# Edge ids broadcast to all partitions by DMA, and a softplus that ends in one instruction, in a graph network kernel

## What is computed

```
h = relu(layernorm(x))
f = (softplus(edge_attr @ W1 + b1) - log 2) @ W2 + b2      # per edge
x = x + segment_sum(h[dst] * f, src)                       # layer 0
h = relu(layernorm(x))
for k in (1, 2):                                           # layer 1, two convolutions
    agg[n, r] = mean of h[src] over the edges with dst = n and type = r
    h = sum over r of agg[:, r] @ Wrel[r] + h @ root + bias    # a relu after the first
x = x + h
```

## Time and profile before

| | us |
|---|---|
| median of 3 runs | 7747.99 (7746.06 to 7757.31) |
| the profiled execution | 7740.94 |
| its span, first to last instruction | 7739.2 |
| busy in the span: PE / PE weight loads | 4879.2 / 3639.4 |
| busy in the span: DVE / ACT / POOL | 3524.5 / 3186.8 / 5938.5 |

### The profile page before, as it was taken

How to read it: one execution, slowest core, us unless ns; L and a number is a source line. 1 busy time by engine, 2 the same in 40 slices (tenths; PEclk the granted TensorE clock), 3 DMA queues, 4 the chain that set the end, 5 groups by cost and what they waited for, 6 DMA issues and landing times. The chain is left out here.

```text
span 7739.2 us, 134678 instructions
## 1 busy us (share of the span) xinstructions
PE 4879.2 (63%) x27214; PEld 3639.4 (47%) x27214; DVE 3524.5 (46%) x10829; ACT 3186.8 (41%) x8459; POOL 5938.5 (77%) x5311
## 2 busy tenths in 40 slices
PE   1877777777777777686666666666644444444444
PEld 1656655665555556544444444444433333333333
DVE  6555555555555555486555555555521111111111
ACT  5555555555555555474333333333322222222222
POOL 4888888888888888846777777777767777777777
PEclk9988888888888888896666666666655555555555
DMA  8555555555555555584222222222222222222222
GB/s 262 86 84 84 84 84 84 84 83 84 84 84 84 84 84 84 70 304 134 70 80 80 78 79 80 77 80 80 77 61 56 56 56 56 56 56 56 56 56 54
DMA packets 587140, 663.53 MB, mean 86 GB/s; under 512 B 109683, under 2 KB 448091, under 8 KB 586755
## 3 DMA queue, kind: packets, MB, share of 16 engines
q0 software_dynamic: 352384, 340.33, 27.3%
q1 hardware_dynamic: 228934, 314.99, 12.9%
q10 hardware_dynamic: 5746, 7.42, 0.4%
HBM read 406.44 MB, written 255.87 MB: 86 GB/s over the span
## 5 line engine op out<-in xcount | busy, mean ns | idle before, releaser
L1321 POOL DMA_INDIRECT got<-table_dram,cidx x3328 | 3150.6, 947 | 1056.0 <-issue 1003.3
L980 POOL DMA_INDIRECT acc_dram<-total,idx x1664 | 2600.2, 1563 | 563.9 <-issue 361.1
L1369 PE MATMUL bank<-got,share 128*128 128x128 f32 x6656 | 1604.4, 417 | 1529.0 <-DMA got<-table_dram,cidx 1493.1
L1369 PEld LDWEIGHTS bank<-got,share 128*128 128x128 f32 x6656 | 1379.0, 307 | 1808.5 <-issue 1702.2
L1423 ACT ACTIVATE share<-cto_node,etcol 128x128 f32<-128x128 bf16 x3328 | 1082.5, 396 | 2756.3 <-PE bank L1369 1863.3
L240 DVE SCALAR_TENSOR_TENSOR xs<-bank,mask_hi,xs 128x128 f32 x416 | 146.0, 351 | 1681.6 <-PE bank L1369 1681.6
L946 DVE TENSOR_TENSOR msg<-bank,factor 128x512 f32<-128x512 f32 x416 | 287.8, 692 | 1219.1 <-issue 889.7
L871 ACT ACTIVATE total<-bank 128x258 f32<-128x258 f32 x832 | 275.5, 384 | 1200.4 <-DMA acc_dram<-total,idx 1200.4
L814 PEld LDWEIGHTS bank<-w,soft 128*128 128x128 f32 x3328 | 569.0, 242 | 33.1
L805 PE MATMUL bank<-msg,same 128*128 128x129 f32 x3328 | 583.9, 328 | 0.7 <-issue 0.7
L797 PE MATMUL bank<-rows,coef 2*128 2x512 bf16 x416 | 170.7, 410 | 653.1 <-DVE same L953 652.7
(11 more groups left out here) (178 smaller groups left out, 7667.1 us busy)
## 6 DMA issues: line engine op xcount, KB each, us to landing
edges<-in_edge_attr SPq DMA_DIRECT2D x415, 256.0 KB
got<-table_dram,cidx POOLq DMA_INDIRECT x3328
table_dram<-made SPq DMA_DIRECT2D x98, 512.0 KB, 3.7
table_dram<-umade SPq DMA_DIRECT2D x98, 512.0 KB, 2.9
win<-split_dram SPq DMA_DIRECT2D x416, 96.0 KB
acc_dram<-total,idx POOLq DMA_INDIRECT x1664, 3.3
acc_dram<-zeros SPq DMA_DIRECT2D x132, 192.0 KB, 2.8
sums<-acc_dram SPq DMA_DIRECT2D x196, 64.0 KB, 3.2
```

The lines of the kernel that those rows point to most:

```text
L980: pool.indirect_dma_start(g.acc_dram[j][:, :], bass.IndirectOffsetOnAxis(ap=idx[k][:, j:j + 1], axis=0), total[k][:, j, 0:F], None, comput ...
L1321: pool.indirect_dma_start(got[k][:, j, :], None, g.table_dram[which][:, :], bass.IndirectOffsetOnAxis(ap=idx[k][:, j:j + 1], axis=0)).then ...
L1369: ins = nc.tensor.matmul(window[k], share[k][:, j, :], got[ka][:, j, :], start=j == 0, stop=j == TG - 1)
```

## The change

The id row reaches all partitions by DMAs that read the same row of DRAM 128 times. In the filter layer the source ids come as int32 from the input itself (`src_row`), and the low parts of the target ids come as bf16 from `rows_dram` (`low`). `to_edge` compares the low part with `want`, the low part of the node number of the partition; within a window of 128 nodes the low parts are distinct. The last group, which the input does not fill, takes its source ids from `last_dram`, which `prepare` writes. The source parts aren't made or stored any more. In the softplus, max(z + b1, 0) = max(z, -b1) + b1: one DVE instruction computes max(z, -b1) + log1p from PSUM, and the missing b1 is added to `neglog`, so that it comes back through the second bias. `bank_z` alternates between two PSUM banks, since the bank is read until that last instruction. The first convolution takes its ids in the same way. For inputs in which a group doesn't fit its window, the matmul for the target stays.

```diff
 # prepare
-            def store_rows(k):
+            def store_rows():
+            sp.wait_ge(s_ids[1], 16 * PIECES)
+            sp.dma_start(g.last_dram.rearrange("(a e) -> a e", a=1), ids[1][QP - 1:QP, EQ - GE:EQ]).then_inc(s_last, 16)
...
             scales(0)
+            dve.wait_ge(s_weights, 16 * 12)
+            v.tensor_scalar(neglog[:, :], neglog[:, :], g.b1c[:, 0:1], None, ALU.add).then_inc(s_neglog, 1)
+            chain(v.tensor_scalar(g.neg_b1[:, :], g.b1c[:, :], -1.0, None, ALU.mult))
...
-            id_parts(1)
             to_floats(1)
...
             chain(v.tensor_copy(g.ctl[:, :], fits[:, :]))
+            chain(v.tensor_scalar(off_f[:, :], g.neg_nid[:, :], -1.0, None, ALU.mult))
+            chain(v.tensor_copy(off_i[:, :], off_f[:, :]))
+            chain(v.tensor_scalar(off_i[:, :], off_i[:, :], P - 1, None, ALU.bitwise_and))
+            chain(v.tensor_copy(g.want[:, :], off_i[:, :]))
 # filter_layer, SP
-                        need(sp, s_dst, s.at(NE - 1))
-                        sp.dma_start(rows[k][:, :, :],
-                                     g.rows_dram[bass.ds(s.at(0), 1)].rearrange("a h d e -> (a h) d e")).then_inc(s_rows[k], 16)
+                        if windows.own:
+                            need(sp, s_hot, s.at(NE - 1))
+                            sp.dma_start(low[k][:, :], g.rows_dram[bass.ds(s.at(0), 1), 1, :].rearrange("a e -> (a e)").partition_broadcast(P)).then_inc(s_rows[k], 16)
...
+                        need(sp, s_same, s.at(NE - 1))
+                        apart(sp, g.gate["sp"])
...
+                            sp.dma_start(src_row[k][:, :], src[bass.ds(s.at(0) * GE, GE)].partition_broadcast(P)).then_inc(s_src_row[k], 16)
 # filter_layer, PE
-                        nc.tensor.matmul(bank_r[:, :], g.coef[0:2, :], rows[s.slot(NE, 2)][0:2, 1, :],
-                                         start=True, stop=True).then_inc(s_src, 1)
-                        need(pe, s_line, s.at(1))
-                        nc.tensor.matmul(bank_z[:, :], g.w1[:, :], edges_t[s.slot(2, 1)][:, :],
+                        need(pe, s_soft, s.at(2) if windows.own else s.at(1))
+                        nc.tensor.matmul(bank_z[s.slot(2, 1) if windows.own else 0][:, :], g.w1[:, :], edges_t[s.slot(2, 1)][:, :],
-                    if s.live(2, NG):
+                    if s.live(2, NG) and not windows.own:
 # filter_layer, ACT
-                        need(act, s_dst, s.at(2) + 1)
-                        need(act, s_hot, s.at(3))
-                        nc.scalar.activation(apart_by[s.slot(2, 2)][:, :], bank_r[:, :], ACT.Identity,
-                                             bias=g.neg_nid[:, bass.ds(s.at(2), 1)]).then_inc(s_apart, 1)
 # filter_layer, DVE
-                        need(dve, s_apart, s.at(2) + 1)
+                        need(dve, s_rows[s.slot(NE, 2)], s.use(NE, 2) * 16 + 16)
                         need(dve, s_pass, s.at(3))
-                        v.tensor_scalar(to_edge[k][:, :, :].rearrange("p a b -> p (a b)"), apart_by[k][:, :], 0.0, None,
-                                        ALU.is_equal).then_inc(s_hot, 1)
+                        v.tensor_scalar(to_edge[k][:, :, :].rearrange("p a b -> p (a b)"), low[s.slot(NE, 2)][:, :],
+                                        g.want[:, bass.ds(s.at(2), 1)], None, ALU.is_equal).then_inc(s_hot, 1)
-                        v.tensor_scalar(soft[s.slot(2, 1)][:, :], bank_z[:, :], g.b1c[:, 0:1], 0.0, ALU.add, ALU.max).then_inc(s_line, 1)
-                        need(dve, s_src, s.at(1) + 1)
+                        need(dve, s_src_row[s.slot(NE, 1)], s.use(NE, 1) * 16 + 16)
                         need(dve, s_total, s.at(2))
-                        v.tensor_tensor(same[k][:, :, :], bank_r[:, :].rearrange("q (p j) -> q j p", j=TG),
+                        v.tensor_tensor(same[k][:, :, :], src_row[s.slot(NE, 1)][:, :].rearrange("q (p j) -> q j p", j=TG),
                                         g.srccol[:, four].unsqueeze(2).to_broadcast([P, TG, P]), ALU.is_equal).then_inc(s_same, 1)
-                        v.tensor_tensor(soft[k][:, :], soft[k][:, :], log1p[k][:, :], ALU.add).then_inc(s_soft, 1)
+                        need(dve, s_e, s.at(2))
+                        v.scalar_tensor_tensor(soft[k][:, :], bank_z[k if windows.own else 0][:, :], g.neg_b1[:, 0:1],
+                                               log1p[k][:, :], ALU.max, ALU.add).then_inc(s_soft, 1)
 # convolve, which = 0
+                    need(sp, s_hot, s.at(3))
+                    sp.dma_start(low[k][:, :], g.rows_dram[bass.ds(s.at(0), 1), 1, :].rearrange("a e -> (a e)").partition_broadcast(P)).then_inc(s_rows[k], 16)
-                    if weigh and s.live(0, NG):
+                    if weigh and s.live(0, NG) and not windows.own:
-                v.tensor_scalar(to_edge[k][:, :, :].rearrange("p a b -> p (a b)"), bank_r[:, :],
-                                g.nid_res[:, bass.ds(entry, 1)], None, ALU.is_equal)
+                if windows.own:
+                    v.tensor_scalar(to_edge[k][:, :, :].rearrange("p a b -> p (a b)"), low[s.slot(4, 1)][:, :],
+                                    g.part[:, 0:1], None, ALU.is_equal)
```

More of the change, by code:

```diff
@@ L133, in __init__ @@
         self.s_got = [nc.alloc_semaphore(f"c_got{k}") for k in range(NGA)]
[L134 removed]
+        self.gate = {name: nc.alloc_semaphore(f"gate_{name}") for name in ("pe", "dve", "pool", "sp")}
         NBX, NT, NG = self.NBX, self.NT, self.NG
@@ L283, in prepare @@
         idt = spare[0:QP, 0:EQ]
-        parts = [sb(f"parts{k}", [QP, 2, EQ], BF16) for k in range(2)]
+        parts = sb("parts", [QP, 2, EQ], BF16)
         span = sb("span", [QP, 2, 4])
@@ L521, in _ @@
             v.memset(zeros[:, :], 0.0).then_inc(s_zero, 1)
-            v.memset(neglog[:, :], -LOG2).then_inc(s_neglog, 1)
+            chain(v.memset(neglog[:, :], -LOG2))
             chain(v.memset(g.eps[:, :], EPS))
             def to_floats(k):
[L526 to L529, removed]
+                if k == 0:
+                    dve.wait_ge(s_parts, 1)
+                if k == 1:
+                    dve.wait_ge(s_last, 16)
+                dve.wait_ge(s_ids[k], 16 * PIECES)
                 v.tensor_copy(idf[k], ids[k][:, :]).then_inc(s_idf, 1)
@@ L537, in group_spans, with dst_parts @@
                 v.tensor_reduce(span[:, 1, :], by_group[1], AX_X, ALU.max).then_inc(s_span, 1)
[L539 to L546, removed]
+            def dst_parts():
+                dve.wait_ge(s_ids[0], 16 * PIECES)
+                chain(v.tensor_scalar(idt, ids[0][:, :], 7, None, ALU.arith_shift_right))
+                chain(v.tensor_copy(parts[:, 0, :], idt))
+                chain(v.tensor_scalar(idt, ids[0][:, :], P - 1, None, ALU.bitwise_and))
+                v.tensor_copy(parts[:, 1, :], idt).then_inc(s_parts, 1)
             def moments(k):
@@ L686, in filter_layer @@
         edges = [sb(f"edges{k}", [P, TG, F]) for k in range(NE)]
-        rows = [sb(f"rows{k}", [2, 2, GE], BF16) for k in range(NE)]
+        rows = [sb(f"rows{k}", [2, GE], BF16) for k in range(NE)]
+        low = [sb(f"low{k}", [P, GE], BF16) for k in range(NE)]
+        src_row = [sb(f"src_row{k}", [P, GE], I32) for k in range(NE)]
         win = [sb(f"win{k}", [P, 3 * F], BF16) for k in range(NE)]
@@ L702, in filter_layer @@
         idx = [sb(f"idx{k}", [P, TG], I32) for k in range(NTO)]
-        bank_t, bank_z, bank_e, bank_r, bank_h = g.bank[0:5]
+        bank_t, bank_e, bank_h = g.bank[0], g.bank[2], g.bank[4]
+        bank_z, bank_r = (g.bank[1], g.bank[3]), g.bank[3]
         bank_c, bank_s = g.bank[5:7], g.bank[7]
@@ L721, in filter_layer @@
         s_ec = sem("f_ec")
-        s_src = sem("f_src")
+        s_src_row = [sem(f"f_src_row{k}") for k in range(NE)]
         s_same = sem("f_same")
         s_dst = sem("f_dst")
-        s_apart = sem("f_apart")
         s_hot = sem("f_hot")
@@ L855, in step @@
                         need(act, s_soft, s.at(2))
-                        nc.scalar.activation(t[:, :], bank_z[:, :], ACT.Abs, bias=g.b1c[:, 0:1]).then_inc(s_abs, 1)
-                    if s.live(2, NG) and windows.own:
-                        need(act, s_dst, s.at(2) + 1)
-                        need(act, s_hot, s.at(3))
-                        nc.scalar.activation(apart_by[s.slot(2, 2)][:, :], bank_r[:, :], ACT.Identity,
-                                             bias=g.neg_nid[:, bass.ds(s.at(2), 1)]).then_inc(s_apart, 1)
+                        nc.scalar.activation(t[:, :], bank_z[s.slot(2, 1) if windows.own else 0][:, :], ACT.Abs, bias=g.b1c[:, 0:1]).then_inc(s_abs, 1)
                     if s.live(1, NG):
@@ L1193, in convolve @@
             rows = [sb(f"crows{k}", [2, GE], BF16) for k in range(4)]
+            low = [sb(f"clow{k}", [P, GE], BF16) for k in range(4)]
             to_edge = [sb(f"cto_edge{k}", [P, P, TG], BF16) for k in range(2)]
@@ L1269, in step @@
                         if now.live(0, NG):
```

(11 more changed lines are left out.)

54 lines of the change are left out of this document (28 added, 26 removed).

## The result

| | before | after |
|---|---|---|
| median, us | 7750.38 (4 runs) | 7832.48 (4 runs) |
| ratio to before | | 1.0101, 95% interval 1.0084 to 1.0119 |
| the profiled execution, us | 7740.94 | 7832.82 |

The forecast was 7761 us, in a range from 7718 to 7812. By the medians the kernel lost 82 us, which puts it above the range. The two profiled executions lie 92 us apart, and what follows is read from these two.

A forecast was written before the change was run, and what follows sets the result against it. POOL, issuing without a pause, was taken as the bound. Terms +14 + 3 - 2 - 2 = +13 us on the profiled 7740.94 gave 7754; the median lies 7.05 above, so 7761 us, range 7718 to 7812.

The forecast's parts named there:

- What bounds the kernel: All three main stages: POOL issues without a pause, 1664 instructions in each; everything else is slack.
- The mechanism that touches POOL: Filter layer: a DVE instruction with two SBUF inputs holds POOL's start, except for its last 0.13 us.
- They have the same length, 0.68 us: Filter layer: `same`, now with two SBUF inputs, takes as long as L959; even phases cost 34 us, 30 taken.
- 16 given back: Filter layer: L959 drops to one SBUF input, so its waits on POOL go; 16 us gained, 25 at most.
- Rival 2: Filter layer: `same` holds POOL where it lies, keeping its distance to POOL's starts; +44 us, 7791; chance 0.27.
- The whole-remainder rule: Filter layer: the skill's rule blocks POOL for the whole remaining 0.40 us of `same`; 83 us, so 7814.
- Rival 4: DMA engines crowded: slow same-row reads or late scatter landings make POOL wait; 208 us if 0.5 late, 7960; chance 0.08.
- Rival 3: Filter layer: later landings put `same` behind POOL's starts and L959's cost goes; -20 to -30 us, 7723; chance 0.20.
- Off the path: Filter layer: work saved on PE, ACT and DVE is covered by POOL's 7.47 us per group; costed at nothing.
- DMA engines: Filter layer: the hardware queue's 17.5% share doubles, total from 57% to about 75%; not a bound, costs nothing.
- Preparation and filling: Before POOL is busy: fewer id-row stores and shorter waits for ACT; -2 us and -2 us.
- First convolution: `to_edge` now reads one bf16 SBUF tile, which can hold POOL too: +3 us (0 to +7).

The follow-up runs named there:

- the run with the extra comparison from PSUM: Kernel before the change, plus a second comparison ahead of `same` that reads its ids from PSUM (`bank_r`), result unused: 7728.70 us, ratio 0.9981.
- The dense order: Changed kernel with `same` written and read in the order in which the ids lie, still two SBUF inputs: 7761.27 us, ratio 1.0020.
- the constant tile's comparison: Kernel before the change, plus an unused second comparison ahead of `same` reading a constant float32 SBUF tile, no DMA added: 7917.98 us, ratio 1.0225.

## Why the prediction was wrong

- **What bounds the kernel**: right. POOL issues almost without a pause in all three stages after the change too (from 300 to 3300 us, 12 of 1564 gaps between scatters are over 0.35 us, 2.7 us in all beyond the usual), and no engine's saved time was worth anything in itself, as the run with the extra comparison from PSUM shows.
- **The mechanism that touches POOL**: right, with the last part of the DVE instruction free as the row showed. Over all waits for L959 the free part is 0.13 us, as the prediction read it from one row. In the long `same` it is 0.18 us, as in the row above (0.89 - 0.71) and as the median of its 188 waits. No start within the new softplus instruction was held, as the prediction said.
- **The step that failed** is the sentence "They have the same length, 0.68 us". I took the length of `same` from the row in which it reads PSUM and kept it for SBUF, and gave no bounds to it. In SBUF, read in steps of 16 bytes, it takes 1.07 us. The cost grows with the square of the length: by the prediction's own formula (1.07 - 0.13)^2 / (2 x 1.867) x 416 = 98 us in place of 34. With 16 given back, +3 and -4, that is +81; measured +82. The closeness is in part luck. The trace has 96 us for `same` from 300 to 3300 us, some 102 for the whole stage, and about 24 given back in place of 16, since `to_node` and `to_edge` happened to cost nothing in the changed kernel. That makes 78 of the scatters' +80, and the profiled execution is 92 us longer, not 82. The dense order, in which the assumed length holds, gave +16 against the +13 of the sum.
- **Rival 2** had the sign and the place, at +44 us, and a chance of 0.27; it too was priced with 0.68 us. Its condition, that `same` keeps one distance to POOL's starts, isn't what happened: about as many starts fall into it as even phases give (205 and 192). The whole-remainder rule, whose price set the top of the range, came near with its +67 by luck. The 188 waits are shorter than the remainder by 0.18 us, and with the true length it would give 1.07^2 / (2 x 1.867) x 416 = 128 us for `same`, which is too much.
- **Rival 4** is out: POOL's idle time before the scatters grew by 5 us in total. Whether the scatters landed later, as forecast, isn't known, since the profile after gives no landing time for them.
- **Rival 3**, lucky phases, happened in small: in the changed kernel `to_node` and `to_edge` cost nothing (8 us before). As a gain of the whole kernel it happened only in the run with the extra comparison from PSUM.
- **Off the path**: right. DVE's busy time did not fall to 1290 us, though, but only to 1540. `same` grew by 0.39 us per group (164 us), the softplus instruction takes 0.743 us in place of 0.69 (22 us) and `to_edge` 0.375 in place of 0.34 (15 us); the last 50 us of the difference were not traced.
- **DMA engines**: 76% as forecast (75%).
- **Preparation and filling**: forecast -4, and the first scatter starts 4 us earlier, at 188.6 us.
- **First convolution**: forecast +3, measured +4; since the second, whose code is the same, shows +3 as well, the change's own part of it may be nothing.

What stays open: why POOL's starts fall more often and earlier into the constant tile's comparison than even phases give. The count shows that they do, and that this and the old sum make up its 175 us; what ties the starts to the comparison was not tried.

## What to carry to other kernels

Where GpSimd issues DMAs without a pause, it is the bound, and a DVE instruction that nobody waits for can still cost: look at where its inputs lie before looking at how long DVE is busy. Where DVE has two inputs, give it at most one in SBUF and the other in PSUM, or keep such instructions short: of two `same` with both inputs in SBUF, the one of 0.68 us cost 22 us and the one of 1.07 us cost 96. One input isn't a safeguard by itself, since `to_edge`, with a single bf16 input in SBUF, held 18 of the 31 starts that fell into it before the change, for 1.4 us in all. And when an operand moves from PSUM to SBUF, its access pattern has to be priced anew: no row of before told its duration.

## What the runs showed of the hardware that I had not expected

- A DVE comparison of 512 values, read from SBUF in steps of 16 bytes, takes 1.06 to 1.10 us, with float32 and with int32 ids; in dense order 0.683 us, and from PSUM in the same steps 0.68 us.
- The hold goes one way in these traces. Of the 391 `same` of the changed kernel 299 began while a scatter was under way. They took 1.073 us on average, against 1.075 us for the others, and none of these scatters got longer either.
- Ids broadcast as 128 reads of the same 1 or 2 KB of DRAM, 384 KB per 7.5 us, cost about 6 us of 7740.
- A useless DVE instruction made the kernel 0.19% faster, only by moving others in time. Differences of 15 us in this kernel can be phases alone.
